# LayerNorm statistics and normalisation of x in one pass over HBM instead of two, in a fused attention and mixture kernel on Trainium2

## The chip, the cores and the metric

The program runs on the 8 cores of one Trainium2 chip. Each core computes one of the 8 sequences of the batch, with no traffic between cores. The metric is device time in microseconds of the slowest core.

## The reference, cut to what matters

Each core has an x of 4096 tokens by 1024 channels. The layer is

```python
xn = _layernorm(x, axis=-1)          # (x - m) / sqrt(v + 1e-5)
s = _L0_attn_ref(xn, Wq, Wk, Wv)     # 16 heads, softmax over all keys, then causal zeroing
g = _silu(_L0_ffn_ref(xn, sim_matrix, gates, q_proj, k_proj, v_proj, o_proj))
x = x + s * g
# in _L0_ffn_ref, the router:
xn = x / jnp.maximum(jnp.linalg.norm(x, axis=-1, keepdims=True), EPS)
sn = sim_matrix / jnp.maximum(jnp.linalg.norm(sim_matrix, axis=0, keepdims=True), EPS)
logits = xn @ sn - jax.nn.sigmoid(gates)
```

The change touches only how the mean m and the variance v of each token, the normalised xn, and from v the reciprocal norm that the router needs, are obtained.

## The kernel before, in words

The program is written engine by engine: one function for each of SyncE (`sync_prog`), TensorE, VectorE (`vector_prog`), ScalarE (`scalar_prog`) and GpSimd. The order on each engine is the order of the code, and semaphores tie the engines together. There are four stages: P0 (LayerNorm, transposes, router), P1 (the mixture's projections, attention and output), P3 (16-head attention, in 8 pairs of heads) and the combination with x, which is interleaved with the last pair of P3.

The change lies in the first part of P0. x is cut into NT = 32 tiles of 128 tokens by 1024 channels, 512 KB each. Before the change P0 goes twice over x:

- First pass. SyncE (L354 to 358) loads tile after tile into two buffers of `stage`. VectorE (L921 to 924) sums each tile into `s1_all`, and ScalarE (L1273 to 1277) squares it and sums the squares into `acc_all`. Tile i may be loaded once both have read tile i-2 (the waits on `vP0a` and `aSQ`).
- Between the passes. VectorE (L926 to 936) makes the means `m_all`, variances `v_all` and `veps` of all tokens; ScalarE (L1279 to 1286) makes `rstd_all` by Ln and Exp, and the reciprocal norm `invr_raw` with VectorE's help (L938 to 942). Then come the small steps for `sim` (L943 to 953, with ScalarE's L1288 to 1291).
- Second pass. SyncE (L361 to 364) loads the 32 tiles again into the same two buffers; tile i may be loaded once VectorE has normalised tile i-2 (the wait on `vXN`). VectorE (L954 to 974) normalises tile i into a half of `xnb` (L958; `xnb` lies in R2, so the rows say R), and copies the transposed tile i-1 out of PSUM into `xnT` (L964, the last one L971). TensorE (L592 to 603) transposes a tile in 8 pieces in between (L599).

After the second pass VectorE casts 24 blocks of projection weights (L982), which GpSimd loads into two buffers (L472): each load from the third on waits for the cast of two blocks before it. The first two of these loads are issued at the program's start. Then TensorE computes the router's logits (L624), VectorE works out the mask for each tile (L992 to 1014), and P1 begins.

Of the kernel before, what the change touches and what calls it, by code (L numbers as in the profile page):

```python
# [9 lines left out]
AF = mybir.ActivationFunctionType  # L10
ALU = mybir.AluOpType
# [191 lines left out]
class Builder:  # L203
# [34 lines left out]
    def alloc(self, st):  # L238
# [58 lines left out]
            "tC2", "aC2", "gC2", "tU2", "vC2", "vC1r",  # L297
# [46 lines left out]
    def sync_prog(self, e):  # L344
# [4 lines left out]
        if "P0" in self.stages:  # L349
            e.dma_start(s.sim_in[:].rearrange("p (a e) -> p a e", a=8),  # L350
                        d["sim"].rearrange("(a p) e -> p a e", p=128)).then_inc(sem["dW"], 16)
            e.dma_start(s.gates_in[0:1, :],
                        d["gates"].rearrange("(a e) -> a e", a=1)).then_inc(sem["dW"], 16)
            for i in range(NT):  # L354
                if i >= 2:
                    e.wait_ge(sem["vP0a"], i - 1)
                    e.wait_ge(sem["aSQ"], i - 1)
                e.dma_start(xb[i % 2], xr[:, i, :]).then_inc(sem["dX0" if i % 2 == 0 else "dX1"], 16)
            e.wait_ge(sem["vP0a"], NT)
            e.wait_ge(sem["aSQ"], NT)  # L360
            for i in range(NT):  # L361
                if i >= 2:
                    e.wait_ge(sem["vXN"], i - 1)
                e.dma_start(xb[i % 2], xr[:, i, :]).then_inc(sem["dX20" if i % 2 == 0 else "dX21"], 16)
# [51 lines left out]
        if "P0" in self.stages:  # L416
            finals.update(dX0=16 * 16, dX1=16 * 16, dX20=16 * 16, dX21=16 * 16,
                          dW=32, dP0=16 * 12, dP1=16 * 12)
# [11 lines left out]
    def debug_dmas(self, e):  # L430
# [17 lines left out]
        if "P0" in self.stages:  # L448
            e.dma_start(d["dbg_mv"][:, 0:32], s.m_all[:]).then_inc(sem["dDbg"], 16)
            e.dma_start(d["dbg_mv"][:, 32:64], s.v_all[:]).then_inc(sem["dDbg"], 16)  # L450
            n += 2
# [459 lines left out]
    def vector_prog(self, e):  # L911
# [4 lines left out]
        if "P0" in self.stages:  # L916
# [4 lines left out]
            for i in range(NT):  # L921
                e.wait_ge(sem["dX0" if i % 2 == 0 else "dX1"], 16 * (i // 2 + 1))
                e.reduce_sum(s.s1_all[:, i:i + 1], xb[i % 2], axis=AX.X
                             ).then_inc(sem["vP0a"], 1)
            e.drain()
            e.tensor_scalar(s.m_all[:], s.s1_all[:], 1.0 / C, None, ALU.mult)  # L926
            e.drain()
            e.tensor_tensor(s.lna[:], s.m_all[:], s.m_all[:], ALU.mult)
            e.wait_ge(sem["aSQ"], NT)
            e.drain()  # L930
            e.scalar_tensor_tensor(s.v_all[:], s.acc_all[:], 1.0 / C, s.lna[:],
                                   ALU.mult, ALU.subtract)
            e.drain()
            e.tensor_scalar(s.veps[:], s.v_all[:], 1.0e-5, None, ALU.add)
            e.drain()
            e.drain().then_inc(sem["vP0b"], 1)
            e.wait_ge(sem["aP0b1"], 1)
            e.tensor_tensor(s.ddt[:], s.lnv[:], s.lna[:], ALU.subtract  # L938
                            ).then_inc(sem["vP0b2"], 1)
            e.wait_ge(sem["aP0b2"], 1)  # L940
            e.tensor_scalar(s.invr_all[:], s.invr_raw[:], 1.0e12, None, ALU.min
                            ).then_inc(sem["vP0b3"], 1)
# [10 lines left out]
                            ALU.mult).then_inc(sem["vSnn3"], 1)  # L953
            for i in range(NT):  # L954
                e.wait_ge(sem["dX20" if i % 2 == 0 else "dX21"], 16 * (i // 2 + 1))
                if i >= 2:
                    e.wait_ge(sem["tTR"], i - 1)
                e.tensor_scalar(s.xnb[:, (i % 2) * 1024:(i % 2) * 1024 + 1024],  # L958
                                xb[i % 2], s.m_all[:, i:i + 1], s.rstd_all[:, i:i + 1],
                                ALU.subtract, ALU.mult).then_inc(sem["vXN"], 1)  # L960
                if i >= 1:
                    e.wait_ge(sem["tTR"], i)
                    slot = PBb[3] if (i - 1) % 2 == 0 else PBb[7]
                    e.tensor_copy(  # L964
                        s.xnT[:].rearrange("p (ct n) -> p ct n", ct=8)
                        [:, :, (i - 1) * 128:i * 128],
                        slot[:].rearrange("p (ct n) -> p ct n", ct=8)
                    ).then_inc(sem["vEv"], 1)
            e.wait_ge(sem["tTR"], NT)
            slot = PBb[3] if (NT - 1) % 2 == 0 else PBb[7]  # L970
            e.tensor_copy(s.xnT[:].rearrange("p (ct n) -> p ct n", ct=8)  # L971
                          [:, :, (NT - 1) * 128:NT * 128],
                          slot[:].rearrange("p (ct n) -> p ct n", ct=8)
                          ).then_inc(sem["vEv"], 1)
            e.wait_ge(sem["tTR"], NT)
# [288 lines left out]
    def scalar_prog(self, e):  # L1264
# [4 lines left out]
        if "P0" in self.stages:  # L1269
            e.wait_ge(sem["dW"], 32)  # L1270
            e.activation(s.sg_row[0:1, :], s.gates_in[0:1, :], AF.Sigmoid
                         ).then_inc(sem["aSg"], 1)
            for i in range(NT):  # L1273
                e.wait_ge(sem["dX0" if i % 2 == 0 else "dX1"], 16 * (i // 2 + 1))
                e.activation(s.xnb[:, (i % 2) * 1024:(i % 2) * 1024 + 1024],
                             xb[i % 2], AF.Square,
                             accum_out=s.acc_all[:, i:i + 1]).then_inc(sem["aSQ"], 1)
            e.wait_ge(sem["vP0b"], 1)
            e.activation(s.lnv[:], s.veps[:], AF.Ln)  # L1279
            e.drain()  # L1280
            e.activation(s.rstd_all[:], s.lnv[:], AF.Exp, scale=-0.5)
            e.activation(s.lna[:], s.v_all[:], AF.Ln, scale=float(C)
                         ).then_inc(sem["aP0b1"], 1)
            e.wait_ge(sem["vP0b2"], 1)
            e.activation(s.invr_raw[:], s.ddt[:], AF.Exp, scale=0.5
                         ).then_inc(sem["aP0b2"], 1)
            e.wait_ge(sem["vSim2"], 1)
            e.activation(s.n2b[0:8, :], s.n2[0:8, :], AF.Ln)  # L1288
            e.drain()
            e.activation(s.invn_r[0:8, :], s.n2b[0:8, :], AF.Exp, scale=-0.5  # L1290
                         ).then_inc(sem["aSim"], 1)
            lgT = s.R3[:, 8192:16384].bitcast(F32)
            for j in range(8):
                e.wait_ge(sem["tL"], j + 1)
                e.copy(lgT[0:8, j * 512:(j + 1) * 512],
                       PB[1][0:8, (j % 2) * 512:(j % 2) * 512 + 512]
                       ).then_inc(sem["aLT"], 1)
            e.wait_ge(sem["vRt1"], 1)
            e.activation(s.expg_all[:], s.gated_all[:], AF.Exp).then_inc(sem["aRt"], 1)
# [79 lines left out]
```

## Time and profile before

| what | value |
|---|---|
| device time, median of 2 runs | 3712.55 us (3712.02 to 3713.09) |
| the profiled execution's own time | 3708.26 us |
| its span, slowest core (core 5) | 3706.7 us |
| spans of the 8 cores | 3690.5 to 3706.7 us |
| granted TensorE clock, core 5 | 0.783 |
| busy: TensorE, VectorE, ScalarE, GpSimd | 70%, 63%, 58%, 7% of the span |

The span runs from the first to the last instruction of the slowest core; the execution's own time is 1.6 us longer. The median of the runs lies 4.3 us above the profiled execution. Times inside the trace are microseconds from the span's start on core 5.

### The profile page before, as it was taken

To read this page: it belongs to the slowest core of one execution; us is meant where nothing else is said; L and a number is where in the kernel's file an instruction comes from. 1 tells how busy PE (TensorE), PEld (TensorE's weight loads), DVE (VectorE), ACT (ScalarE), POOL (GpSimd) and SP (SyncE) were. 2 spreads that over 40 slices of the span, in tenths; PEclk is the share of its full clock that TensorE was granted. 3 is DMA by queue.
4 is the path that set the end of the run, shared out by engine and by line. 5 is a ranking of instruction groups with operands and counts; after the bars stand their busy time and mean duration, and the time that the engine had idled before them with its cause. 6 is when DMAs were issued, how large, how long until landed. Compare 5 with 4: busy or idle time off the path is not lost.

```text
span 3706.7 us, 60449 instructions; the slowest of 8 cores (3690.5 to 3706.7 us)
## 1 busy us (share of the span) xinstructions
PE 2578.4 (70%) x18642; PEld 1160.7 (31%) x18642; DVE 2317.7 (63%) x6185; ACT 2156.4 (58%) x2500; POOL 254.3 (7%) x706
## 2 busy tenths in 40 slices
PE   0312999876738877877788777777788777876551
PEld 0201444333313333333333333333333333332220
DVE  3526777503325677667667766766766776776664
ACT  3000000162104789679779868877977977897662
POOL 0020000000000001001000100100100100011112
PEclk9996999888978776886777787687678778765555
DMA  6550000001140000000000000000000000002446
GB/s 182 177 140 1 1 1 1 1 1 71 52 162 1 4 4 7 3 4 7 4 3 6 6 4 4 7 3 4 7 4 3 6 5 4 4 7 78 132 139 197
DMA packets 40390, 133.94 MB, mean 36 GB/s; under 512 B 6290, under 2 KB 6290, under 8 KB 40082
## 3 DMA queue, kind: packets, MB, share of 16 engines
q1 hardware_dynamic: 27346, 88.12, 7.4%
q0 software_dynamic: 12736, 41.95, 3.9%
q8 instruction: 163, 2.67, 0.3%
q14 instruction: 145, 1.19, 0.1%
HBM read 96.50 MB, written 33.55 MB: 35 GB/s over the span
## 4 chain that ended last, share of the span: by engine, by line
PE 32%; ACT 20%; DVE 18%; issue 15%; DMA 10%; DVEq 4%; POOL 1%; ACTq 0%; SPq 0%; POOLq 0%
ACT expC L1329 6%; ACT stagef L1344 6%; PE PB L886 5%; DMA stagef<-x 5%; PE PB L900 5%; PE PB L871 5%; DVE cacc L1069 4%; PE PB L800 4%; PE PB L803 3%; PE PB L815 3%; PE PB L758 3%; ACT stagef L1329 3%; ACT R L1344 3%; DVE tmpc L1193 2%; DVE stagef L1069 2%
## 5 line engine op out<-in xcount | busy, mean ns | idle before, releaser
L1193 DVE TENSOR_REDUCE tmpc<-stagef 128x2 f32<-128x1024 bf16 (+2 forms) x726 | 811.3, 1126 | 238.7 <-ACT stagef L1344 180.5
L1329 ACT ACTIVATE expC<-PB 128x1024 bf16<-128x1024 f32 x768 | 863.1, 1124 | 87.0 <-PE PB L886 86.9
L1344 ACT ACTIVATE stagef<-PB 128x1024 bf16<-128x1024 f32 x600 | 675.3, 1125 | 206.6 <-PE PB L900 132.1
L1193 DVE TENSOR_REDUCE tmpc<-R 128x2 f32<-128x1024 bf16 (+2 forms) x362 | 406.1, 1122 | 118.9 <-ACT R L1344 89.8
L1329 ACT ACTIVATE stagef<-PB 128x1024 bf16<-128x1024 f32 x384 | 434.2, 1131 | 72.3 <-PE PB L886 72.3
L886 PE MATMUL PB<-R 64*128 64x512 bf16 x1152 | 297.4, 504 | 234.7 <-ACT stagef L1344 140.3
L686 PE MATMUL PB<-R,xnT 128*128 128x512 bf16 x1536 | 341.4, 383 | 74.0 <-DVE qk_tmp L1069 72.6
L886 PE MATMUL PB<-QTt,KTt 64*128 64x512 bf16 x1152 | 287.3, 487 | 143.2 <-ACT stagef L1344 76.8
L1344 ACT ACTIVATE R<-PB 128x1024 bf16<-128x1024 f32 x296 | 333.9, 1128 | 82.6 <-PE PB L900 59.5
L1309 ACT ACTIVATE expC<-PB 128x512 bf16<-128x512 f32 x144 | 83.2, 597 | 407.4 <-PE PB L726 406.6
L900 PE MATMUL PB<-R 64*128 64x512 bf16 (+3 forms) x1088 | 263.2, 476 | 39.1 <-ACT expC L1329 20.5
L900 PE MATMUL PB<-KTt,QTt 64*128 64x512 bf16 (+3 forms) x1088 | 254.1, 458 | 44.0 <-ACT expC L1329 24.9
L800 PE MATMUL PB<-xnT,R 128*128 128x512 bf16 x512 | 217.2, 424 | 53.5 <-DVE R L1138 50.9
L686 PEld LDWEIGHTS PB<-R,xnT 128*128 128x128 bf16 x1536 | 147.3, 98 | 256.8 <-issue 93.6
L803 PE MATMUL PB<-xnT,R 128*128 128x512 bf16 x512 | 213.8, 418 | 0.0
L886 PEld LDWEIGHTS PB<-R 64*128 64x128 bf16 x1152 | 72.9, 98 | 392.1 <-issue 388.0
L871 PE MATMUL PB<-R,expC 128*128 128x65 bf16 x2680 | 184.7, 222 | 15.4 <-DVEq L1261 15.4
L871 PE MATMUL PB<-Vau,expC 128*128 128x65 bf16 x2680 | 180.7, 219 | 13.9 <-DVEq L1261 13.9
L871 PEld LDWEIGHTS PB<-R,expC 128*128 128x128 bf16 x2680 | 133.8, 114 | 134.0 <-issue 134.0
L871 PEld LDWEIGHTS PB<-Vau,expC 128*128 128x128 bf16 x2680 | 130.5, 112 | 128.2 <-issue 128.2
L516 POOL TENSOR_SCALAR_AFFINE_SELECT mask<-expC 128x128 bf16<-128x128 bf16 x304 | 81.1, 290 | 1198.1 <-ACT expC L1329 1120.4
L886 PEld LDWEIGHTS PB<-QTt,KTt 64*128 64x128 bf16 x1152 | 72.4, 97 | 290.3 <-issue 286.3
(165 smaller groups left out, 3064.6 us busy)
## 6 DMA issues: line engine op xcount, KB each, us to landing
stagef<-x SPq DMA_DIRECT2D x96, 512.0 KB, 4.4
out<-Vau SPq DMA_DIRECT2D x32, 512.0 KB, 3.6
g_sp<-stagef SPq DMA_DIRECT2D x32, 256.0 KB, 2.0
s_sp<-s_stage POOLq DMA_DIRECT2D x64, 128.0 KB, 2.4
QTt<-g_sp POOLq DMA_DIRECT2D x32, 256.0 KB, 5.7
KTt<-s_sp POOLq DMA_DIRECT2D x32, 256.0 KB, 5.8
R<-qp POOLq DMA_DIRECT2D x8, 512.0 KB, 5.5
R<-kp POOLq DMA_DIRECT2D x8, 512.0 KB, 5.0
```

The costliest lines, as they stand in the source:

```text
L686: last = e.matmul(PB[pb][:, half * 512:(half + 1) * 512], s.xnT[:, ct * 4096 + qt * 128: ct * 4096 + (qt + 1) * 128], src[:, ct * 1024 + h ...
L758: last = e.matmul(pbo[:, half * 512:(half + 1) * 512], aoT[qt % 2][:, ei * 128:(ei + 1) * 128], op_r[:, ei * 1024 + half * 512: ei * 1024 ...
L800: e.matmul(POOL[it["slot"]][:, 0:512], Wq[:, ct * 1024 + pp * 128: ct * 1024 + (pp + 1) * 128], mv, start=(ct == 0), stop=(ct == 7), skip_ ...
L803: last = e.matmul(POOL[it["slot"]][:, 512:1024], Wk[:, ct * 1024 + pp * 128: ct * 1024 + (pp + 1) * 128], mv, start=(ct == 0), stop=(ct == 7),
L815: last = e.matmul(POOL[it["slot"]][:, 0:512], Wv[:, ct * 1024 + pp * 128: ct * 1024 + (pp + 1) * 128], mv, start=(ct == 0), stop=(ct == 7) ...
L871: e.matmul(PB[2][:, h * 512 + qt * 128: h * 512 + qt * 128 + 65], stat, Vau[:, t * 130 + h * 65: t * 130 + h * 65 + 65], start=first, stop ...
L886: last = e.matmul(POOL[it["slot"]][:, h * 512:h * 512 + 512], stat, mv, start=True, stop=True, tile_position=(64 * h, 0))
L900: last = e.matmul(POOL[it["slot"]][:, h * 512:h * 512 + kw], statq, mvk, start=True, stop=True, tile_position=(64 * h, 0))
L1069: e.scalar_tensor_tensor(out, PB[pb][:, ei * 128:(ei + 1) * 128], mask[:, qt * 8 + ei:qt * 8 + ei + 1], acc[:], ALU.mult, ALU.add).then_in ...
L1193: e.tensor_reduce(s.tmpc[:].rearrange("p (h c) -> p h c", h=2)[:, :, c:c + 1], s.c1scr((m1 - 1) % 3)[:, 0:2 * kw] .rearrange("p (h k) -> p ...
L1329: e.activation(s.expCs(es), PB[[0, 1, 3][it["slot"]]][:, :], AF.Exp).then_inc(sem["aC2"], 1)
L1344: e.activation(scr[:, 0:1024], pbsrc[:, 0:1024], AF.Exp).then_inc(sem["aC1"], 1)
```

## The change

P0 goes over x once. SyncE loads 32 tiles instead of 64, into three buffers instead of two. VectorE takes the statistics of a tile with two BN_STATS (one for each half of 512 channels) and one BN_AGGR, which writes mean and variance side by side into `Dup`. After every second tile it adds eps to two variances (`veps`), and ScalarE makes the two `rstd` columns from them by Ln and Exp. VectorE normalises tile i-2 (`emit_xn`) and evacuates the transposed tile i-3 (`emit_ev`) behind the statistics of tile i. ScalarE's squares are gone. The steps for `sim` now stand ahead of the pass, and those for the reciprocal norm behind it. Tile i may be loaded once tile i-3 is normalised.

```diff
--- before.py
+++ after.py
...
+            xb3 = [s.stage[:, 0:1024], s.stage[:, 1024:2048], s.stage[:, 2048:3072]]
+            dxs = ["dX0", "dX1", "dX20"]
             for i in range(NT):
-                if i >= 2:
-                    e.wait_ge(sem["vP0a"], i - 1)
-                    e.wait_ge(sem["aSQ"], i - 1)
-                e.dma_start(xb[i % 2], xr[:, i, :]).then_inc(sem["dX0" if i % 2 == 0 else "dX1"], 16)
-            e.wait_ge(sem["vP0a"], NT)
-            e.wait_ge(sem["aSQ"], NT)
-            for i in range(NT):
-                if i >= 2:
-                    e.wait_ge(sem["vXN"], i - 1)
-                e.dma_start(xb[i % 2], xr[:, i, :]).then_inc(sem["dX20" if i % 2 == 0 else "dX21"], 16)
+                if i >= 3:
+                    e.wait_ge(sem["vXN"], i - 2)
+                e.dma_start(xb3[i % 3], xr[:, i, :]).then_inc(sem[dxs[i % 3]], 16)
...
-            for i in range(NT):
-                e.wait_ge(sem["dX0" if i % 2 == 0 else "dX1"], 16 * (i // 2 + 1))
-                e.reduce_sum(s.s1_all[:, i:i + 1], xb[i % 2], axis=AX.X
-                             ).then_inc(sem["vP0a"], 1)
-            e.drain()
-            e.tensor_scalar(s.m_all[:], s.s1_all[:], 1.0 / C, None, ALU.mult)
-            e.drain()
-            e.tensor_tensor(s.lna[:], s.m_all[:], s.m_all[:], ALU.mult)
-            e.wait_ge(sem["aSQ"], NT)
-            e.drain()
-            e.scalar_tensor_tensor(s.v_all[:], s.acc_all[:], 1.0 / C, s.lna[:],
-                                   ALU.mult, ALU.subtract)
-            e.drain()
-            e.tensor_scalar(s.veps[:], s.v_all[:], 1.0e-5, None, ALU.add)
-            e.drain()
-            e.drain().then_inc(sem["vP0b"], 1)
-            e.wait_ge(sem["aP0b1"], 1)
-            e.tensor_tensor(s.ddt[:], s.lnv[:], s.lna[:], ALU.subtract
-                            ).then_inc(sem["vP0b2"], 1)
-            e.wait_ge(sem["aP0b2"], 1)
-            e.tensor_scalar(s.invr_all[:], s.invr_raw[:], 1.0e12, None, ALU.min
-                            ).then_inc(sem["vP0b3"], 1)
...
+            xb3 = [s.stage[:, 0:1024], s.stage[:, 1024:2048], s.stage[:, 2048:3072]]
+            dxs = ["dX0", "dX1", "dX20"]
+            mvD = s.Dup[:].rearrange("p (i two) -> p two i", two=2)
+            bn6 = s.tmpc[:, 0:12]
+
+            def emit_xn(j):
+                e.wait_ge(sem["aRS"], j // 2 + 1)
+                if j >= 2:
+                    e.wait_ge(sem["tTR"], j - 1)
+                e.tensor_scalar(s.xnb[:, (j % 2) * 1024:(j % 2) * 1024 + 1024],
+                                xb3[j % 3], s.Dup[:, 2 * j:2 * j + 1],
+                                s.rstd_all[:, j:j + 1],
+                                ALU.subtract, ALU.mult).then_inc(sem["vXN"], 1)
+
+            def emit_ev(j):
+                e.wait_ge(sem["tTR"], j + 1)
+                slot = PBb[3] if j % 2 == 0 else PBb[7]
+                e.tensor_copy(
+                    s.xnT[:].rearrange("p (ct n) -> p ct n", ct=8)
+                    [:, :, j * 128:(j + 1) * 128],
+                    slot[:].rearrange("p (ct n) -> p ct n", ct=8)
+                ).then_inc(sem["vEv"], 1)
+
             for i in range(NT):
-                e.wait_ge(sem["dX20" if i % 2 == 0 else "dX21"], 16 * (i // 2 + 1))
+                e.wait_ge(sem[dxs[i % 3]], 16 * (i // 3 + 1))
+                e.bn_stats(bn6[:, 0:6], xb3[i % 3][:, 0:512])
+                e.bn_stats(bn6[:, 6:12], xb3[i % 3][:, 512:1024])
+                e.drain()
+                e.bn_aggr(s.Dup[:, 2 * i:2 * i + 2], bn6)
+                e.drain()
+                if i % 2 == 1:
+                    g = i // 2
+                    e.tensor_scalar(s.veps[:, 2 * g:2 * g + 2],
+                                    mvD[:, 1, 2 * g:2 * g + 2], 1.0e-5, None,
+                                    ALU.add)
+                    e.drain().then_inc(sem["vM"], 1)
                 if i >= 2:
-                    e.wait_ge(sem["tTR"], i - 1)
-                e.tensor_scalar(s.xnb[:, (i % 2) * 1024:(i % 2) * 1024 + 1024],
-                                xb[i % 2], s.m_all[:, i:i + 1], s.rstd_all[:, i:i + 1],
-                                ALU.subtract, ALU.mult).then_inc(sem["vXN"], 1)
-                if i >= 1:
-                    e.wait_ge(sem["tTR"], i)
-                    slot = PBb[3] if (i - 1) % 2 == 0 else PBb[7]
-                    e.tensor_copy(
-                        s.xnT[:].rearrange("p (ct n) -> p ct n", ct=8)
-                        [:, :, (i - 1) * 128:i * 128],
-                        slot[:].rearrange("p (ct n) -> p ct n", ct=8)
-                    ).then_inc(sem["vEv"], 1)
-            e.wait_ge(sem["tTR"], NT)
-            slot = PBb[3] if (NT - 1) % 2 == 0 else PBb[7]
-            e.tensor_copy(s.xnT[:].rearrange("p (ct n) -> p ct n", ct=8)
-                          [:, :, (NT - 1) * 128:NT * 128],
-                          slot[:].rearrange("p (ct n) -> p ct n", ct=8)
-                          ).then_inc(sem["vEv"], 1)
-            e.wait_ge(sem["tTR"], NT)
+                    emit_xn(i - 2)
+                if i >= 3:
+                    emit_ev(i - 3)
+            emit_xn(NT - 2)
+            emit_ev(NT - 3)
+            emit_xn(NT - 1)
+            emit_ev(NT - 2)
+            emit_ev(NT - 1)
+            e.wait_ge(sem["aP0b1"], 1)
+            e.tensor_tensor(s.ddt[:], s.lnv[:], s.lna[:], ALU.subtract
+                            ).then_inc(sem["vP0b2"], 1)
+            e.wait_ge(sem["aP0b2"], 1)
+            e.tensor_scalar(s.invr_all[:], s.invr_raw[:], 1.0e12, None, ALU.min
+                            ).then_inc(sem["vP0b3"], 1)
...
-            for i in range(NT):
-                e.wait_ge(sem["dX0" if i % 2 == 0 else "dX1"], 16 * (i // 2 + 1))
-                e.activation(s.xnb[:, (i % 2) * 1024:(i % 2) * 1024 + 1024],
-                             xb[i % 2], AF.Square,
-                             accum_out=s.acc_all[:, i:i + 1]).then_inc(sem["aSQ"], 1)
-            e.wait_ge(sem["vP0b"], 1)
-            e.activation(s.lnv[:], s.veps[:], AF.Ln)
-            e.drain()
-            e.activation(s.rstd_all[:], s.lnv[:], AF.Exp, scale=-0.5)
-            e.activation(s.lna[:], s.v_all[:], AF.Ln, scale=float(C)
-                         ).then_inc(sem["aP0b1"], 1)
-            e.wait_ge(sem["vP0b2"], 1)
-            e.activation(s.invr_raw[:], s.ddt[:], AF.Exp, scale=0.5
-                         ).then_inc(sem["aP0b2"], 1)
             e.wait_ge(sem["vSim2"], 1)
             e.activation(s.n2b[0:8, :], s.n2[0:8, :], AF.Ln)
             e.drain()
             e.activation(s.invn_r[0:8, :], s.n2b[0:8, :], AF.Exp, scale=-0.5
                          ).then_inc(sem["aSim"], 1)
+            mvD = s.Dup[:].rearrange("p (i two) -> p two i", two=2)
+            for g in range(16):
+                e.wait_ge(sem["vM"], g + 1)
+                e.activation(s.lnv[:, 2 * g:2 * g + 2],
+                             s.veps[:, 2 * g:2 * g + 2], AF.Ln)
+                e.drain()
+                e.activation(s.rstd_all[:, 2 * g:2 * g + 2],
+                             s.lnv[:, 2 * g:2 * g + 2], AF.Exp, scale=-0.5
+                             ).then_inc(sem["aRS"], 1)
+            e.activation(s.lna[:], mvD[:, 1, :], AF.Ln, scale=float(C)
+                         ).then_inc(sem["aP0b1"], 1)
+            e.wait_ge(sem["vP0b2"], 1)
+            e.activation(s.invr_raw[:], s.ddt[:], AF.Exp, scale=0.5
+                         ).then_inc(sem["aP0b2"], 1)
```

Left out of the diff are the names of the two new semaphores and a debug output. TensorE's and GpSimd's programs are as they were.

SyncE's DMA queue, at the program's start, before (x is the input, stagef the buffers; xN at a row's end is how often it repeats):

```order
L358 DMA stagef<-x 128x1024 x2
L358 DMA stagef<-x 128x1024 [waits vP0a,aSQ] x30
L364 DMA stagef<-x 128x1024 [waits vP0a,aSQ]
L364 DMA stagef<-x 128x1024
L364 DMA stagef<-x 128x1024 [waits vXN] x30
```

The same place now:

```order
L350 DMA sim_in<-sim 128x8x8
L352 DMA gates_in<-gates 1x8
L359 DMA stagef<-x 128x1024 x3
L359 DMA stagef<-x 128x1024 [waits vXN] x29
L366 DMA g_sp<-stagef 128x1024 [waits bar,aS4]
```

62 loads that waited for a reader have become 29, all of them released by VectorE's normalisation of the tile three before.

VectorE, the beginning of the second pass, before (R is `xnb`, PB is PSUM; dX20 and dX21 are the landings of x):

```order
L958 TENSOR_SCALAR R<-stagef,m_all,rstd_all 128x1024 [waits dX20]
L958 TENSOR_SCALAR R<-stagef,m_all,rstd_all 128x1024 [waits dX21]
L964 COPY xnT<-PB 128x8x128 [waits tTR]
L958 TENSOR_SCALAR R<-stagef,m_all,rstd_all 128x1024 [waits dX20,tTR]
L964 COPY xnT<-PB 128x8x128 [waits tTR]
L958 TENSOR_SCALAR R<-stagef,m_all,rstd_all 128x1024 [waits dX21,tTR]
L964 COPY xnT<-PB 128x8x128 [waits tTR]
```

VectorE in the one pass now, iterations 4 and 5 (dX1 and dX20 are the landings of tiles 4 and 5, L935 normalises tiles 2 and 3, L943 evacuates tiles 1 and 2):

```order
L951 BN_STATS tmpc<-stagef 128x6 [waits dX1]
L952 BN_STATS tmpc<-stagef 128x6
L954 BN_AGGR Dup<-tmpc 128x2
L935 TENSOR_SCALAR R<-stagef,Dup,rstd_all 128x1024 [waits aRS,tTR]
L943 COPY xnT<-PB 128x8x128 [waits tTR]
L951 BN_STATS tmpc<-stagef 128x6 [waits dX20]
L952 BN_STATS tmpc<-stagef 128x6
L954 BN_AGGR Dup<-tmpc 128x2
L958 TENSOR_SCALAR veps<-Dup 128x2
L935 TENSOR_SCALAR R<-stagef,Dup,rstd_all 128x1024 [waits aRS,tTR]
L943 COPY xnT<-PB 128x8x128 [waits tTR]
```

The normalisation that frees a buffer (L935) now stands behind the statistics of another tile, and in front of the wait for the tile that is loaded into the freed buffer (the dX at the next L951).

## Rows read from the trace of the kernel before

**Rows 1.** Busy time by stretch: both passes, the weight casts, the router.
```profile
core 5: us, PE busy (x) PEld busy (x) DVE busy (x) ACT busy (x) POOL busy (x), PEclk, DMA share, GB/s
8.00:100.00 92.00, 0.00 (x0) 0.00 (x0) 39.15 (x33) 36.85 (x64) 0.00 (x0) 1.00 0.62 184
109.00:197.00 88.00, 32.95 (x266) 25.55 (x266) 46.63 (x67) 0.00 (x0) 0.26 (x1) 1.00 0.60 179
197.00:264.00 67.00, 0.00 (x0) 0.00 (x0) 14.17 (x20) 0.00 (x0) 18.38 (x22) 1.00 0.61 163
264.00:370.00 106.00, 29.85 (x144) 12.90 (x144) 62.56 (x396) 5.03 (x9) 0.77 (x1) 0.67 0.02 6
```
**Rows 2.** Waits, 0 to 200 us: who waited for whom, us, times, longest.
```profile
DVE s_all L923 <- DMA stagef<-x: 58.5, 31, 5.8
...
DVE R L958 <- DMA stagef<-x: 39.7, 27, 3.3
```
**Rows 3.** Chain of waits in the second pass: start, us, what.
```profile
109.17 0.81 DVE R L958
110.01 0.04 issue
110.05 3.75 DMA stagef<-x
...
113.97 0.82 DVE R L958
...
170.87 6.37 DMA stagef<-x
...
178.30 3.78 DMA stagef<-x
```
**Rows 4.** DMA issues of the page: count, KB, median us from issue to landing.
```profile
stagef<-x SPq DMA_DIRECT2D x96, 512.0 KB, 4.4
out<-Vau SPq DMA_DIRECT2D x32, 512.0 KB, 3.6
```
**Rows 5.** Timeline around the end of the first pass: start, us, engine, line, operation.
```profile
98.58 1.22 DVE L923 TENSOR_REDUCE s_all<-stagef 128x1 f32<-128x1024 f32 x1 [1.84 <-DMA stagef<-x]
...
99.90 0.18 DVE L926 TENSOR_SCALAR m_all<-s_all 128x32 f32<-128x32 f32 x1
...
100.16 0.19 DVE L928 TENSOR_TENSOR lna<-m_all 128x32 f32<-128x32 f32 x1
...
101.04 1.28 ACT L1279 ACT_TABLE_LOAD   x1 [1.32 <-DVEq L936]
102.33 0.23 ACT L1279 ACTIVATE lnv<-veps 128x32 f32<-128x32 f32 x1
102.63 0.23 ACT L1281 ACTIVATE rstd_all<-lnv 128x32 f32<-128x32 f32 x1
...
103.08 0.19 DVE L938 TENSOR_TENSOR ddt<-lnv,lna 128x32 f32<-128x32 f32 x1 [2.20 <-ACT lna L1282]
...
103.81 1.21 DVE L944 COPY R<-PB 8x1024 f32<-8x1024 f32 x1
```
**Rows 6.** Timeline at the program's start.
```profile
5.06 1.86 PE L589 MATMUL PB<-idt_f,sim_in 128*8 128x128 f32 x8 [5.06 <-DMA gates_in<-gates]
```
**Rows 7.** Timeline of VectorE at the end of the second pass.
```profile
190.22 0.81 DVE L958 TENSOR_SCALAR R<-stagef,m_all,rstd_all 128x1024 bf16<-128x1024 f32 x1 [1.20 <-DMA stagef<-x]
190.95 0.68 DVE L964 COPY xnT<-PB 128x1024 bf16<-128x1024 bf16 x1
...
192.71 0.81 DVE L958 TENSOR_SCALAR R<-stagef,m_all,rstd_all 128x1024 bf16<-128x1024 f32 x1 [1.08 <-DMA stagef<-x]
...
194.89 0.69 DVE L971 COPY xnT<-PB 128x1024 bf16<-128x1024 bf16 x1 [0.77 <-PE PB L599]
195.50 1.28 DVE L982 CAST R<-R 128x1024 bf16<-128x1024 f32 x2
```

More of the change, by code:

```diff
@@ L296, in alloc @@
             "tC1", "aC1", "vC1",
-            "tC2", "aC2", "gC2", "tU2", "vC2", "vC1r",
+            "tC2", "aC2", "gC2", "tU2", "vC2", "vC1r", "vM", "aRS",
             "vCM",
@@ L416, in sync_prog @@
         if "P0" in self.stages:
-            finals.update(dX0=16 * 16, dX1=16 * 16, dX20=16 * 16, dX21=16 * 16,
+            finals.update(dX0=16 * 11, dX1=16 * 11, dX20=16 * 10,
                           dW=32, dP0=16 * 12, dP1=16 * 12)
@@ L448, in debug_dmas @@
         if "P0" in self.stages:
-            e.dma_start(d["dbg_mv"][:, 0:32], s.m_all[:]).then_inc(sem["dDbg"], 16)
-            e.dma_start(d["dbg_mv"][:, 32:64], s.v_all[:]).then_inc(sem["dDbg"], 16)
-            n += 2
+            e.dma_start(d["dbg_mv"][:, 0:64], s.Dup[:]).then_inc(sem["dDbg"], 16)
+            n += 1
         e.wait_ge(sem["dDbg"], 16 * n)
```

## The prediction

> **What bounds the kernel now.** I read the busy time by stretch first. The change touches the first 195 us of 3707; behind them the same instructions follow in the same order. In the two passes [rows 1] the reader is to see that no engine is full: VectorE is busy 39 of 92 us in the first and 47 of 88 us in the second, and the DMA engines move 184 and 179 GB/s at a share of 0.6. Next the waits [rows 2]: VectorE waits 58.5 us in the first pass and 39.7 us in the second, each time for a tile of x to land. So both passes go at the pace of the transfers.
>
> Then the chain of waits [rows 3], for how a transfer and its buffer hang together. A normalisation begins at 109.17, the load that it releases is issued at 110.05 and takes 3.75 us to land, and the next use of landed data begins at 113.97. Between issue and use lie 3.75 + 0.17 us. With two buffers this loop is walked once per two tiles, and so the passes cost 92/32 = 2.9 and 88/32 = 2.75 us per tile [rows 1]. The quantity to watch is how many loads are under way at a time, and what else stands in the loop.
>
> **The change, step by step.** I compare the moment at which VectorE starts its first weight cast, 195.50 before [rows 7]. From there on nothing differs: each weight load is released by a cast, only the first two are there from the start in either kernel, and TensorE waits for the casts' end or VectorE's copies as before. A shift of this moment is a shift of the end.
>
> *Start.* The sim steps now come first. TensorE's transposes of sim end at 5.06 + 1.86 = 6.92 [rows 6], so the copy starts at 7.0. From this copy to the first normalisation it was 109.17 - 103.81 = 5.36 us [rows 3, 5]. The table load of 1.28 us [rows 5], which lay ahead of it, now falls inside, since ScalarE's first Ln stands there. The loop starts at 7.0 + 5.36 + 1.28 = 13.6. The first three loads are issued at the start; they are hidden behind this.
>
> *Statistics.* No row shows BN_STATS. The nearest is the sum over 1024 fp32 values, 1.22 us [rows 5]. Two instructions over 512 each read the same data; I take 1.22 + 0.08 for the second one's start = 1.3 us. The bounds: half of it, 0.65, if it ran at twice the rate, and 2.6, if it needed two passes over the data. BN_AGGR is tiny: a tiny operation with its drain takes 100.16 - 99.90 = 0.26 us [rows 5]; with the drain ahead of it 0.34. Every second tile adds `veps` and a drain, 0.27, so 0.14 per tile. Sum 1.78 per tile.
>
> *The loop.* This is the step that decides. VectorE in iteration i waits for tile i, takes its statistics, and normalises tile i-2. The load of tile i waits for the normalisation of tile i-3, which stands in iteration i-1, directly ahead of the wait for tile i; between them there is only one evacuation. So in spite of three buffers only one load is under way at a time: the other two buffers hold tiles i-1 and i-2, whose statistics are done but which aren't normalised yet. Nothing but the evacuation of 0.68 us [rows 7] lies beside the transfer. The period is
>
> - 0.04 for the issue after the normalisation and 3.75 for the load [rows 3]. I take this row since its load was issued while no other was under way, as all will be. The bounds are 3.6, the shortest of the page's medians for 512 KB on this queue, and 4.4, the median of loads of x, mostly with a second one beside them [rows 4];
> - 0.17 from landing to the next instruction [rows 3];
> - 1.78 for the statistics;
> - 0.08 for the two waits and 0.84 for the normalisation [rows 3].
>
> That is 6.66 us per tile, against 2.9 + 2.75 = 5.65 for the two passes together. Half the loads are gone, but each has lost its partner, and the statistics that lay beside a transfer now lie in series with it.
>
> By the Trainium skill (DMA: Bandwidth & Descriptors, Anatomy of one DMA) a transfer costs some 2.0 us fixed plus its bytes at 436 GB/s, which is an estimate of 3.2 us for 512 KB. By this the period would be 6.11 and the sum below 16 us smaller. The row of 3.75 is against it, and no row of x shows less than that.
>
> *ScalarE.* The two squares of the first pass go; they were hidden (beside VectorE's sums). The Ln and Exp of a pair take 0.23 each and start some 0.3 apart [rows 5]. The pair's first `rstd` is needed by VectorE a whole iteration later, so they are hidden. Were they not (a wait at every pair), it would be 0.6 x 16 = 10 us. Ln and Exp needed one table load for both [rows 5], so none is added in the loop.
>
> *TensorE.* It transposes one tile per 6.7 us; 8 transposes take some 1 us and the evacuation reads them an iteration later. Hidden. The granted clock stood at 1.00 in the second pass and in the casts' stretch behind it, in which TensorE did nothing [rows 1]; I expect no other clock from the sparser transposes, and these aren't on the path.
>
> *The sum.* Iterations 0 and 1 take 1.64 + 0.1 and 1.64 + 0.27 + 0.1 = 3.75, iteration 2 up to the end of the first normalisation 1.64 + 0.1 + 0.84 = 2.6: 13.6 + 3.75 + 2.6 = 20.0. Then come 29 periods, tile 3 to 31: 29 x 6.66 = 193.1, so 213.1 is the end of the normalisation of tile 29. Tail: evacuation 28, normalisation 30, evacuation 29 take 0.6 + 0.73 + 0.68 = 2.0; from the last normalisation to the first cast it was 195.50 - 192.71 = 2.8 [rows 7]; and the steps for the reciprocal norm, now here, take 103.81 - 103.08 = 0.7 [rows 5]. The first cast starts at 213.1 + 5.5 = 218.6, which is 23.1 us later than 195.50.
>
> On the profiled execution's own 3708.3 us this gives 3731.4; the median of the runs stands 4.3 us higher, and on it the sum gives 3735.7. I say 3733, between the two. The core then moves only half of the bytes in the same time (16.8 MB instead of 33.6), which if anything shortens the loads. The Trainium skill (DMA: Bandwidth & Descriptors, Latency and other measured facts) says that lighter HBM load lowers a transfer's fixed cost; the case of before has no lightly loaded stretch of such loads to show it.
>
> **The rivals.**
>
> *A: the overlap works.* If loads ran ahead, the pass would be VectorE-bound: statistics 1.78, normalisation 0.77 and evacuation 0.68 make some 3.25 us per tile. The transfers, at 2.75 us per tile with two under way, would be hidden. 29 x (6.66 - 3.25) = 99 us less: the first cast at 119.6, 76 us earlier than before, and the kernel at 3712.6 - 76 = 3637. For it: VectorE has room in both passes [rows 1] and there are three buffers. Against it: the order of the code. A load can't be issued before its buffer's normalisation, and that one stands one evacuation ahead of the wait. 0.04.
>
> *B: a lone load is much quicker.* The shift of 23.1 us is gone if the period is 23.1/29 = 0.8 us shorter, with a load landing in 2.95 us instead of 3.75; the time is then that of before, 3713, and 3724 if it comes half way. For it: the engines moved 184 GB/s at a share of 0.62 [rows 1], which is 297 GB/s while busy or 1.8 us for 512 KB, so 2 us of a load are no data; and the other cores' demand halves too. Against it: 3.75 at 110.05 and 3.78 at 178.30 [rows 3], each after a gap. 0.13. The Trainium skill's 3.2 us, cited above, would lie in this case, at 3733 - 16 = 3717.
>
> *C: the statistics cost double.* This rival ends slower. BN_STATS needs two passes over its data, 2.6 us a pair instead of 1.3. All of it lies in series with the loads, so it costs in full: 32 x 1.3 = 42 us more, 3775. It needs a pair to take 1.3 + 1.6 = 2.9 us, or the same rise in the loads, for the loss to pass 2%. For it: no row prices the instruction, and a load once took 6.37 us [rows 3]. Against it: every VectorE reduction and copy of fp32 in these rows goes at about one value per ns. 0.06.
>
> **How the numbers follow.** The likeliest case (one load at a time, at the rows' prices) has 0.77. Its own range is 3.6 to 4.4 us a load and -0.1 to +0.2 us for the statistics, which is -4 - 3 and +19 + 6 around 3733: 3726 to 3758. For 8 in 10 I take in the upper part of B below and stop short of C above: 3714 to 3760. A measurement of this kernel can tell about 2% from no change, 74 us here. Faster by over that needs A with a bit of luck: 0.02. Slower by over that needs C and slower loads together: 0.02. Within 2%: 0.96.
>
> **What would show it.** In the profile after: the loads of x in P0 never overlap, and each is issued right behind L935 of the tile three before; VectorE waits for x some 29 times, about 3.2 us each (3.92 less the evacuation), 94 us in all; ScalarE and TensorE are never what L935 or L943 wait for; the DMA share is around 0.3 and some 78 GB/s in a stretch of the pass; the first cast starts near 219 and the spacing behind it is as before. I am wrong if two loads are seen under way in the steady pass (then A), if the loads take 3.3 us or less (B), or if a BN_STATS takes over 1 us (C).

## The result, and the profile after

| what | before | after |
|---|---|---|
| median, see below | 3713.4 us (7 of 10 runs) | 3740.4 us (7 of 11 runs) |
| median of all runs | 3715.4 us | 3742.9 us |
| ratio after / before | | 1.0068, 95% interval 1.0056 to 1.0080 |
| profiled execution | 3708.3 us | 3740.7 us |
| spans of the cores | 3690.5 to 3706.7 | 3715.0 to 3739.1 |

The kernel got slower by 0.68%, some 25 us (21 to 30 by the interval), and so no change at 2%. Some executions of any kernel are slow, with a lower granted clock on the cores of one die or both, so the first row, the ratios and the times in the table of experiments leave them out, and the profile is that of another execution of the changed kernel without this.

The busy time by stretch, of the slowest core (core 2) of the changed kernel: the pass in two parts, the weight casts, the router. It answers to [rows 1].

```profile
core 2: us, PE busy (x) PEld busy (x) DVE busy (x) ACT busy (x) POOL busy (x), PEclk, DMA share, GB/s
8.00:100.00 92.00, 12.86 (x106) 9.98 (x106) 41.46 (x76) 4.54 (x17) 0.00 (x0) 1.00 0.29 87
100.00:213.00 113.00, 16.18 (x128) 12.38 (x128) 47.84 (x88) 3.25 (x16) 0.00 (x0) 1.00 0.24 75
230.00:298.00 68.00, 0.00 (x0) 0.00 (x0) 14.93 (x22) 0.00 (x0) 19.44 (x22) 1.00 0.64 163
302.00:406.00 104.00, 31.32 (x144) 13.47 (x143) 63.27 (x399) 5.02 (x9) 0.00 (x0) 0.64 0.00 1
```

Two passes of 92 and 88 us have become one of over 200. In it VectorE is busy 45% and 42% of the time, against 43% and 53% in the two passes before, and the DMA share has halved, from 0.6 to 0.24 to 0.29. No engine and no queue is full: something goes in turns. The granted clock is 1.00 through the pass and the casts, as before, and 0.64 in the router's stretch against 0.67.

The waits of the same core from 0 to 230 us (who waited for whom, us, times, longest), which answer to [rows 2]:

```profile
PE PB L593 <- DVE R L935: 188.1, 32, 13.1
DVE tmpc L951 <- DMA stagef<-x: 107.1, 29, 5.4
...
DVE R L935 <- issue: 6.6, 28, 0.3
```

VectorE stood still for 107.1 us until x landed, 29 times, once for each load that waits for a buffer; that is more than the 58.5 + 39.7 us of two passes before. And the chain of waits over two tiles (start, us, what), which answers to [rows 3]:

```profile
60.75 0.82 DVE R L935
61.57 0.02 issue
61.59 0.02 SPq L358
61.61 0.03 issue
61.63 4.15 DMA stagef<-x
65.78 0.03 issue
65.81 0.02 DVEq L950
65.83 0.04 issue
65.87 0.69 DVE tmpc L951
66.57 0.59 DVEq L953
67.16 0.07 issue
67.23 0.21 DVE Dup L954
...
67.52 0.17 DVE veps L958
...
67.95 0.82 DVE R L935
...
68.83 3.77 DMA stagef<-x
...
72.70 0.69 DVE tmpc L951
...
74.48 0.82 DVE R L935
...
75.37 4.00 DMA stagef<-x
```

The chain never leaves the loop: normalisation, load, statistics, normalisation. Each load is issued 0.06 or 0.07 us after a normalisation has ended, and the next one only after this one has been used. From normalisation to normalisation it is 7.20 us (60.75 to 67.95, with the `veps` step) and 6.53 us (67.95 to 74.48, without).

The queue's view of the loads (L359) and the end of the pass on VectorE:

```profile
L359 SPq DMA_DIRECT2D stagef<-x x32: 327/328/432, 2.1 to 216.1; - x32
...
DMA to landing us min/median/max: 3.5/4.1/9.7
```

```profile
18.54 0.81 DVE L935 TENSOR_SCALAR R<-stagef,Dup,rstd_all 128x1024 bf16<-128x1024 f32 x1
...
222.72 0.81 DVE L935 TENSOR_SCALAR R<-stagef,Dup,rstd_all 128x1024 bf16<-128x1024 f32 x1 [0.26 <-issue]
...
229.01 1.30 DVE L983 CAST R<-R 128x1024 bf16<-128x1024 f32 x2
```

The first normalisation starts at 18.54, that of tile 29 at 222.72: 29 periods of 7.04 us. The first cast is at 229.01 here, against 195.50 [rows 7].

This first cast is the ruler for all experiments, as it is free of what happens in the 3500 us behind it. I take its mean over the 8 cores, from each core's VectorE instructions: 195.2 before (191.3 to 198.3) and 223.9 after (218.6 to 229.0), which is 28.7 us later. What lies between the first cast and the end of the core is 3502.5 us before and 3504.9 after, on the same mean. So nearly the whole loss arises in the pass; the total has its noise on top. The ruler has noise, too: in the other profile of the changed kernel it is 226.9, with loads that took 0.1 us longer on the mean, so a difference of some 3 us between two runs says nothing.

### The profile page after: what moved, and what is told of

Read it like the earlier page. It is cut to its first block, busy times and chain, and to the rows that moved or that the text cites. A ratio compares the mean times of both kernels' runs of the same rounds, so it can differ in the third digit from the quotient of the medians.

```text
span 3798.1 us, 60465 instructions; the slowest of 8 cores (3754.3 to 3798.1 us)
## 1 busy us (share of the span) xinstructions
PE 2661.5 (70%) x18642; PEld 1177.9 (31%) x18642; DVE 2333.8 (61%) x6261; ACT 2125.2 (56%) x2466; POOL 255.8 (7%) x706
## 4 chain that ended last, share of the span: by engine, by line
PE 39%; ACT 20%; issue 14%; DVE 12%; DMA 9%; DVEq 4%; POOL 1%; ACTq 0%; SPq 0%; POOLq 0%
PE PB L680 10%; ACT stagef L1345 7%; ACT expC L1330 6%; PE PB L880 5%; DMA stagef<-x 4%; PE PB L894 4%; PE PB L794 4%; PE PB L865 4%; PE PB L797 3%; PE PB L752 3%; ACT stagef L1330 3%; PE PB L809 3%; DVE tmpc L1194 3%; ACT R L1345 3%; DMA KTt<-s_sp 2%
## 5 line engine op out<-in xcount | busy, mean ns | idle before, releaser
L680 PE MATMUL PB<-R,xnT 128*128 128x512 bf16 x1536 | 391.0, 423 | 72.0 <-DVE qk_tmp L1070 71.1
L894 PE MATMUL PB<-KTt,QTt 64*128 64x512 bf16 (+3 forms) x1088 | 258.3, 466 | 39.7 <-ACT expC L1330 18.1
L794 PE MATMUL PB<-xnT,R 128*128 128x512 bf16 x512 | 220.3, 430 | 55.1 <-DVE R L1139 50.7
L680 PEld LDWEIGHTS PB<-R,xnT 128*128 128x128 bf16 x1536 | 161.8, 106 | 287.0 <-issue 238.9
L797 PE MATMUL PB<-xnT,R 128*128 128x512 bf16 x512 | 218.9, 428 | 0.0
L593 PE MATMUL PB<-idt_bf,R 128*128 128x128 bf16 x256 | 32.4, 306 | 188.7 <-DVE R L935 188.7
```

The lines of the kernel that those rows point to most:

```text
L680: last = e.matmul(PB[pb][:, half * 512:(half + 1) * 512], s.xnT[:, ct * 4096 + qt * 128: ct * 4096 + (qt + 1) * 128], src[:, ct * 1024 + h ...
L794: e.matmul(POOL[it["slot"]][:, 0:512], Wq[:, ct * 1024 + pp * 128: ct * 1024 + (pp + 1) * 128], mv, start=(ct == 0), stop=(ct == 7), skip_ ...
L797: last = e.matmul(POOL[it["slot"]][:, 512:1024], Wk[:, ct * 1024 + pp * 128: ct * 1024 + (pp + 1) * 128], mv, start=(ct == 0), stop=(ct == 7),
L894: last = e.matmul(POOL[it["slot"]][:, h * 512:h * 512 + kw], statq, mvk, start=True, stop=True, tile_position=(64 * h, 0))
```

## The experiments

Ten runs. Seven kernels were timed several times beside the kernel before and have a ratio to it, with its 95% interval; the other three have one profiled run. The first cast of each is the mean over its 8 cores, and the time is the median as above:

| run | what differs | first cast | us | ratio to before |
|---|---|---|---|---|
| after again | nothing | 223.9 | 3740.7 | |
| statistics twice | two more BN_STATS per tile | 260.3 | 3774.8 | 1.0134 (1.0077 to 1.0191) |
| normalise first | order on VectorE | 135.9 | 3652.1 | 0.9822 (0.9772 to 0.9872) |
| four buffers | one more buffer | 127.4 | 3670.2 | 0.9855 (0.9787 to 0.9922) |
| half load | 256 KB a tile | 191.6 | 3708.8 | |
| before, lone loads | one load under way in pass 2 | 267.5 | 3780.6 | |
| copy on ScalarE | three buffers, evacuation on ScalarE | 226.3 | 3737.1 | 1.0060 (1.0007 to 1.0114) |
| four buffers, copy on ScalarE | both | 127.4 | 3635.0 | 0.9814 (0.9704 to 0.9923) |
| four buffers, normalise first | both | 127.4 | 3640.7 | 0.9809 (0.9782 to 0.9836) |
| the same, copy on ScalarE | all three | 109.9 | 3616.0 | 0.9790 (0.9740 to 0.9841) |

The five faster kernels are clear of no change, but each of their intervals reaches across 2%, so none is shown to be faster by more than 2%.

**The changed kernel again.**

> The changed kernel once more, for one undisturbed profile. My account (one load of x under way at a time, in series with the statistics and the normalisation) expects the period of the pass at 7.0 us, loads of 4.0 us, the first weight cast at 228, which is 33 us later than before, and 3735 to 3745 in all. As the total rose by only 25 to 27 us, some 6 to 8 us must come back behind the first cast: the stretches behind it (router, P1, P3) are to be compared with before, at the same clock.

The period was 7.04 us on the slowest core, and that core's first cast came 33.5 us later than the slowest core's before. But what I expected to come back behind it did not exist: this core needs 3510.1 us from the cast to its end, and the slowest of before 3511.2. I had read the shift off one core of one profile. Over the cores the shift is 28.7 us, and this lies within the 21 to 30 us of the timed runs. The cores differ by how long their loads take: the median load was 3.6 us on core 0, whose first cast is at 218.6, and 4.0 on core 2 with 229.0.

**Statistics twice.** Is the statistics' time in series with the load?

```diff
                 e.bn_stats(bn6[:, 6:12], xb3[i % 3][:, 512:1024])
+                e.bn_stats(s.tca[:, 0:6], xb3[i % 3][:, 0:512])
+                e.bn_stats(s.tca[:, 6:12], xb3[i % 3][:, 512:1024])
```

> The two BN_STATS of each tile are issued a second time, into a scratch tile. If the statistics lie in series with the load (my account), each tile costs 1.29 us more and the whole 32 x 1.29 = 41 us: 3784. If the pass were bound by the transfers or had slack beside them (rival: the loads set the pace and VectorE's work is hidden), nothing: 3743.

```profile
59.73 0.69 DVE L951 BATCH_NORM_STATS2 tmpc<-stagef 128x6 f32<-128x512 f32 x1 [3.48 <-DMA stagef<-x]
60.34 0.68 DVE L952 BATCH_NORM_STATS2 tmpc<-stagef 128x6 f32<-128x512 f32 x1
60.94 0.68 DVE L953 BATCH_NORM_STATS2 tca<-stagef 128x6 f32<-128x512 f32 x1
61.53 0.68 DVE L954 BATCH_NORM_STATS2 tca<-stagef 128x6 f32<-128x512 f32 x1
```

This is VectorE's timeline of one tile of that run. The extra pair takes 0.60 + 0.59 us from start to start, less than the 1.29 that I had put, so 38 us for 32 tiles. The first cast came 36.4 us later; the time rose by 34 us between the medians, and by 0.66% or 25 us between the ratios, whose interval here is wide (1.0077 to 1.0191). The wait for x in front of the tile is still 3.48 us: VectorE, idle for half the pass, couldn't hide one instruction in it. The rival that expected nothing is out.

**Normalise first.** Same three buffers, same instructions; only what stands ahead of the wait differs.

```diff
             for i in range(NT):
+                if i >= 2:
+                    emit_xn(i - 2)
+                if i >= 3:
+                    emit_ev(i - 3)
                 e.wait_ge(sem[dxs[i % 3]], 16 * (i // 3 + 1))
...
-                if i >= 2:
-                    emit_xn(i - 2)
-                if i >= 3:
-                    emit_ev(i - 3)
```

> Three buffers as they are; only the order on VectorE changes: iteration i normalises tile i-2 and evacuates tile i-3 first, and then waits for tile i. The load of tile i+1 is then released ahead of the wait for tile i, so two are under way. By my account a loop over two tiles holds one load of 4.3, 0.2 to its use, 2.05 of statistics, 0.84 of normalisation and some 0.4 for rstd, 7.8 us or 3.9 per tile: 29 x (7.0 - 3.9) = 90 us less, 3652. The rival that three buffers are too few, or that BN_STATS and the order are not what matters and the loads alone are slow, expects no more than 10 us.

The first cast moved from 223.9 to 135.9, 88 us, and the time to 3652.1. The waits of its slowest core from 0 to 120 us:

```profile
DVE R L935 <- ACT rstd_all L1285: 10.7, 14, 0.8
DVE tmpc L955 <- DMA stagef<-x: 7.4, 14, 1.1
```

The wait for x is down to 1.1 us at most, though a load has not become shorter (median 4.1 us). A new wait has come up, for `rstd`: the normalisation of an even tile now follows the statistics of the second tile of its pair at once, and Ln and Exp show with 0.8 us. This run settles the case: moving two instructions per tile ahead of the wait, and nothing else, turns the loss into a gain of 1.8% (1.3 to 2.3).

**Four buffers.** The order of the changed kernel, one more buffer.

```diff
-                if i >= 3:
-                    e.wait_ge(sem["vXN"], i - 2)
-                e.dma_start(xb3[i % 3], xr[:, i, :]).then_inc(sem[dxs[i % 3]], 16)
+                if i == 3:
+                    e.wait_ge(sem["vSnn3"], 1)
+                if i >= 4:
+                    e.wait_ge(sem["vXN"], i - 3)
+                e.dma_start(xb3[i % 4], xr[:, i, :]).then_inc(sem[dxs[i % 4]], 16)
```

> The order of the changed kernel, but a fourth buffer (tile i may be loaded once tile i-4 is normalised; the first load into it waits for the sim steps, which use that space). Two loads are under way. By my account two periods are one load of 4.3 + 0.2 + 2.05 + 0.84 = 7.4 us, 3.7 per tile: 96 us less, 3647. If the third buffer was not the limit (rival), no change: 3743. If two loads under way make each other so slow that the sum stays (rival of bandwidth), the loads read over 6 us.

The first cast was at 127.4, 96.5 us earlier. Its total of 3670.2 has a wide spread (3639 to 3689), and the profile shows why the ruler is better: from cast to end its cores took 3515 us on the mean, 10 more than the changed kernel's, in code that is the same, and its cores 0 to 3 had a granted clock of 0.771 to 0.774 where cores 4 to 7 had 0.782 to 0.785. The spans of the latter four (median 3634.5) lie 94.5 us below those of the same cores of the changed kernel (3729.0). Loads read 3.9 us, though nearly every one overlapped another; the rival that two make each other slow is out, too.

**Half load.** What is a load made of?

```diff
-                e.dma_start(xb3[i % 3], xr[:, i, :]).then_inc(sem[dxs[i % 3]], 16)
+                hw = 1024 if i < 3 else 512
+                e.dma_start(xb3[i % 3][:, 0:hw], xr[:, i, 0:hw]).then_inc(sem[dxs[i % 3]], 16)
```

This kernel leaves out the second 512 channels of every tile from the fourth on; all computation runs on what the buffer holds.

> From tile 3 on only the first 512 of 1024 channels are loaded (256 KB instead of 512), the rest of the buffer keeps older data; all other work stays. It measures what part of the load is bytes, and whether the load lies in series. Serial account: the load falls from 4.0 us to 4.0 minus the time of 256 KB. At 297 GB/s, the rate of the busy DMA engines before the change, that is 0.9 us, 26 us over 29 periods, P0's first cast near 200. If a load were all fixed cost (rival), no change, 224; if it were all bytes, 2.0 us each and 58 us in all.

The first cast came at 191.6, 32.3 us earlier, or 1.11 us for each of 29 periods. The median load of a core fell from 3.6 to 4.1 us to 2.6 to 2.8 us:

```profile
stagef<-x SPq DMA_DIRECT2D x29, 256.0 KB, 2.8
```

So 256 KB more or less are 1.11 us, a rate of 236 GB/s, and 2.7 - 1.1 = 1.6 us of a load would be independent of its size. The latter is an estimate that takes the time as linear in the bytes; two sizes can't test that, and the noise of the ruler allows 1.0 to 1.2 us for the 256 KB. I had expected 0.9 us; both rivals (all fixed, all bytes) missed by more. What the load gives up (from 3.91 to 2.80 us on the mean of all loads), the pass gives up one for one.

**Before, with lone loads.** What does it cost the old kernel to lose its second load under way?

```diff
-                if i >= 2:
-                    e.wait_ge(sem["vXN"], i - 1)
+                if i >= 1:
+                    e.wait_ge(sem["vXN"], i)
```

> The kernel before, with one edit: in its second pass a load waits for the normalisation of the tile just before it, so that one load is under way instead of two, and nothing else is added. My account (what the change lost is the second load under way) expects 0.04 + 4.0 + 0.17 + 0.84 = 5.05 us per tile in that pass instead of 2.75: 32 x 2.3 = 74 us more, 3716 + 74 = 3790, first weight cast at 269. Should lone loads be much quicker than paired ones (3.2 us or less), it would be under 50 us more.

The chain of waits in its second pass:

```profile
149.69 0.82 DVE R L958
150.57 3.85 DMA stagef<-x
154.59 0.82 DVE R L958
155.47 4.05 DMA stagef<-x
159.69 0.82 DVE R L958
```

5.0 us per tile, first cast at 267.5, 72.3 us later than before. With nothing else changed, the loss of the partner costs 2.3 us a tile. It is the larger part of what eats the gain of the single pass: the other is the statistics in series, 1.9 us. By this account 29 periods cost 29 x (2.3 + 1.9) = some 120 us more than tiles of the second pass, and some 90 us are gone, as the first normalisation starts at 18.54 and not at 109.17; some 30 us remain, and 28.7 were measured. The load, 3.85 to 4.05, is the one that the changed kernel has too.

**The copy on ScalarE.** `emit_ev` moved from VectorE to ScalarE, behind Ln and Exp of the next pair, once with three buffers and once with four. The first part of the edit is VectorE's, the second ScalarE's.

```diff
-                if i >= 3:
-                    emit_ev(i - 3)
...
+                if g >= 1:
+                    emit_ev(2 * g - 2)
+                    emit_ev(2 * g - 1)
```

> The changed kernel, but ScalarE instead of VectorE copies the transposed tiles out of PSUM. In the changed kernel this copy of 0.68 us lies beside the load, so taking it off VectorE is worth nothing in the loop and at most 2 us at the tail: 3741 to 3745. A rival in which VectorE's total work sets the pace expects 32 x 0.68 = 22 us less.

> Fourth buffer and the copy on ScalarE together. With four buffers two loads are under way and VectorE's work of 1.93 + 0.84 + 0.68 = 3.45 us per tile lies close to the pass's pace of 3.6 (first cast at 127 on the mean of the cores). Without the copy VectorE has 2.8 us per tile, but the loop of load 4.1 + 0.2 + 1.93 + 0.84 over two tiles, 3.55 us, stays. So I expect at most 3 us less than with four buffers alone, first cast at 124 to 127 and 3640 to 3650; if VectorE bound that pass (rival), 0.7 us per tile, 20 us less.

Neither made the pass shorter: 226.3 against 223.9 with three buffers, which is within the noise of the ruler, and 127.4 against 127.4 with four. VectorE's time was not the bound in either; in the latter it waits about 1 us for each of these two tiles:

```profile
62.48 0.69 DVE L944 BATCH_NORM_STATS2 tmpc<-stagef 128x6 f32<-128x512 f32 x1 [1.28 <-DMA stagef<-x]
...
66.39 0.69 DVE L944 BATCH_NORM_STATS2 tmpc<-stagef 128x6 f32<-128x512 f32 x1 [1.02 <-DMA stagef<-x]
```

**Both, and the version that beats the two kernels.** Four buffers with the normalisation first; then with the copy on ScalarE as well.

> Four buffers and the normalisation ahead of the wait for the next tile, both; the copy stays on VectorE. Three loads are under way. The loop of the load then no longer binds, and VectorE should: 1.93 + 0.73 + 0.62 = 3.3 us per tile from start to start, and some 0.3 for the wait for rstd that is now exposed at every second tile (0.77 in the run with three buffers and this order): 3.6. That is the pace that four buffers alone reached (3.53), so by my account no gain on it: first cast at 125 to 130. A rival in which the loop of the load still binds expects 7 us less or more by the loads' length.

> The same with the copy on ScalarE. VectorE has 1.93 + 0.81 + 0.35 = 3.1 us per tile, and the transfers ran at 2.75 us per tile with two under way before the change. With the bound on VectorE I expect 3.1 per tile, 29 x (3.53 - 3.1) = 12 us less than with four buffers alone, first cast at 113 to 118, and 3635 to 3640. If the loads bind at a common rate whatever is under way, first cast stays at 127.

The first gave 127.4, as expected. Not three loads are under way in it, as I had put, but two at most, as a load of 3.8 us is hardly longer than a tile's 3.5. The wait for x is gone from the list of waits of its slowest core from 0 to 115 us; what is left in the pass is

```profile
DVE R L937 <- ACT rstd_all L1287: 10.8, 14, 0.8
DVE R L937 <- issue: 3.2, 13, 0.6
```

VectorE with its wait for `rstd` is now the bound, and over the cores the first casts lie within 1.1 us of each other (126.7 to 127.8), where the loads had spread them by 10 us in the changed kernel. So taking the copy off it counts now, which it didn't before. VectorE's timeline of the last version:

```profile
60.78 0.81 DVE L937 TENSOR_SCALAR R<-stagef,Dup,rstd_all 128x1024 bf16<-128x1024 f32 x1 [0.22 <-issue]
...
64.09 0.81 DVE L937 TENSOR_SCALAR R<-stagef,Dup,rstd_all 128x1024 bf16<-128x1024 f32 x1 [0.77 <-ACT rstd_all L1284]
...
66.59 0.81 DVE L937 TENSOR_SCALAR R<-stagef,Dup,rstd_all 128x1024 bf16<-128x1024 f32 x1 [0.22 <-issue]
```

Two tiles take 66.59 - 60.78 = 5.81 us, 2.9 per tile, where I had put 3.1, and the first cast is at 109.9, below the 113 to 118 that I gave. The kernel takes 3616.0 us, some 20 less than I expected, and 0.979 of before (0.974 to 0.984); against the changed kernel it takes off 114 us at the ruler. The rival of a common rate of the loads is out: they follow down to 2.9 us.

## Why the prediction was right

The forecast was 3733, in a range of 3714 to 3760, slower by 0.6%; measured were 3740.4 and a ratio of 1.0068. Step by step, on the slowest core:

- *Start.* Put at 20.0 for the end of the first normalisation; it ended at 18.54 + 0.81 = 19.35. The table load did move into this stretch.
- *Statistics.* Put at 1.78 + 0.08 for the waits = 1.86. Measured from L951 to L935: 67.95 - 65.87 = 2.08 with `veps` and 74.48 - 72.70 = 1.78 without, 1.93 on the mean. Case C, a doubled price, is out: one BN_STATS over 512 values takes 0.68 us and the next starts 0.61 later. What I had too little here (0.07) I had too much between landing and use (0.17 put, 0.09 measured).
- *The loop.* One load at a time, in series with the statistics, was right. Every load in the chain follows a normalisation by 0.06 us. Three experiments show it independently: doubled statistics cost in full, a halved load pays in full, and the place of the normalisation alone is worth 88 us.
- *The load* is the term that was mis-sized. I took 3.75 from one row for a load issued alone. With the period of 7.04, less 1.93, 0.82, 0.06 and 0.09 (landing to L951), it is 4.1 us on this core, and with the mean first cast of 223.9 some 3.95 over all. 29 x 0.2 to 0.35 us are 6 to 10 us too few, and the measured time lies 7 us above mine. The row was also less alone than I had read it: the load at 110.05 got a partner 0.7 us later (the next one in the trace is issued at 110.77), and when the other row, 178.30, was issued, the load before it was still under way to 178.46. Loads that were alone to their end took 3.9 us on the mean. I had taken a single low row where the medians of the trace stood at 4.3 to 4.4; half way would have hit.
- *Tail.* Put at 5.5; it is 229.01 - 223.53 = 5.5.
- *What would show it.* I gave 29 waits and 94 us; there were 29 and 107.1, by the longer loads. 78 GB/s and a share of 0.3: 75 to 87 and 0.24 to 0.29. ScalarE and TensorE, which I had put at never, appear once each among what L935 and L943 wait for, with 0.6 and 0.8 us.

Case A (3637) was out by the order of the code, and the experiment with this order turned round came to 3652. Case B needed loads of 2.95 us, or some of the way there. The loads came out longer than my 3.75, not shorter, though all cores asked for less, and the remark that half of the bytes would if anything shorten them did not come true against that figure. In the old kernel with lone loads, which moves 103 GB/s in that pass on its slowest core, the median was 3.9; in the changed kernel with 75 to 87 GB/s it was 3.6 to 4.1, by core. The Trainium skill's estimate of 3.2 us (DMA: Bandwidth & Descriptors, Anatomy of one DMA) was too low for 512 KB; for 256 KB the same formula gives an estimate of 2.6, and 2.6 to 2.8 was measured. That section gives its fit for transfers that GpSimd issues, while these loads are SyncE's, on the hardware queue, with all 8 cores loading. Here, by the estimate above, the fixed part came out at 1.6 us and not 2.0, and the bytes went at 236 GB/s and not at 436.

## What to carry to other kernels

Count the loads that are under way, not the buffers: a buffer counts only from the instruction that frees it, and what matters is how much of the loop stands between that instruction and the wait for the next load. A deeper pipeline on the computing side (statistics of i, normalisation of i-2) holds buffers longer and can eat the one that it was given; freeing first and waiting afterwards cost here no more than 10.7 us of waits for `rstd` in 120 us, against 88 us gained; a fourth buffer did the same work. When a pass shows every engine under half busy, ask for the loop; moving work off an engine pays only once that loop is gone, as the copy on ScalarE did: nothing with three buffers, nothing with four, 17.5 us at the first cast with four buffers and the order mended.

## What the runs showed of the hardware that was not expected

A load of 512 KB alone on its core took 3.6 to 4.1 us at the median, by core, against 4.2 to 4.4 in the second pass of before, where a second one was under way at 179 GB/s. In the last version, with two under way and some 180 GB/s, the mean was 4.1 where loads that were alone had 3.9. So with a second load under way each took only 4 to 12% longer. Cores of one run differ: 3.6 us on one and 4.1 on another, which over 29 serial loads spread the first cast by 10 us (218.6 to 229.0), where the paired loads of before had spread it by 7. What decides which core gets the short loads was not tried. In each of the 12 profiles the core with the shortest median load had an even number, and in the old kernel with lone loads the even cores had 3.7 to 3.8 and the odd ones 3.9; but the slowest core of the changed kernel, 2, is even as well.
